# Experts' remainder in units of 64 rows: 14 tiles of 128 rows and 7 of 64 in turns, where 21 tiles of 128 stood

## The reference

```
x = x + tanh(g_xattn) * cross_attention(layernorm(x), ctx)      # |scores|, softmax, 16 heads
logits = layernorm(x) @ w_router                                 # 8 experts
top 2 of softmax(logits) per token, their probabilities as weights
h = gelu(layernorm(x) @ w1[e] + b1[e])                           # 256 -> 1024
y = h @ w2[e] + b2[e]                                            # 1024 -> 256
x = x + tanh(g_ffn) * sum over the two chosen experts of weight * y
```

## Time and profile before

| what | value |
|---|---|
| time, median of 3 runs | 653.47 us (652.01 to 654.26) |
| the profiled execution | 654.93 us, its span 653.1 us |
| PE busy | 633.6 us (97%) |
| DVE, ACT, POOL busy | 459.7, 333.8, 310.7 us |
| mean granted TensorE clock | 0.989 |
| chain of waits, by engine | PE 57%, DMA 3%, DVE 2% |

### The profile page before, as it was taken

The page is one execution under the profiler, slowest core; times in us unless marked ns, Lnnn a source line. Parts: engine busy times, 40 slices in busy tenths (PEclk is TensorE's granted clock), DMA queues, the critical chain, the costliest instruction groups (busy, mean ns, idle before and its releaser), DMA issues.

```text
span 653.1 us, 20940 instructions
## 1 busy us (share of the span) xinstructions
PE 633.6 (97%) x6637; PEld 562.7 (86%) x6638; DVE 459.7 (70%) x1298; ACT 333.8 (51%) x741; POOL 310.7 (48%) x420
## 2 busy tenths in 40 slices
PE   8999999999999999899999999999999999999993
PEld 7799999999999999798888888888888888888872
DVE  5687888888888896689665656556564647777773
ACT  4668777788778875623242323323242324444441
POOL 6423477777777455766352323334242433333333
PEclk9899999999999999899999999999999999999997
DMA  6144354555544445524954333333433344533322
GB/s 208 41 135 156 115 159 153 164 164 177 165 149 132 147 156 172 117 55 81 202 74 60 50 49 49 51 51 58 60 46 56 43 58 54 56 54 52 52 35 25
DMA packets 89157, 63.37 MB, mean 97 GB/s; under 512 B 51489, under 2 KB 84775, under 8 KB 88935
## 3 DMA queue, kind: packets, MB, share of 16 engines
q1 hardware_dynamic: 75519, 43.95, 26.0%
q0 software_dynamic: 13440, 18.14, 16.5%
q10 hardware_dynamic: 104, 0.04, 0.0%
HBM read 28.08 MB, written 24.63 MB: 81 GB/s over the span
## 4 chain that ended last, share of the span: by engine, by line
PE 57%; DMA 3%; DVE 2%; issue 1%; POOLq 0%; ACT 0%; SPq 0%; DVEq 0%; ACTq 0%
PE banks L1720 20%; PE banks L1703 20%; PE banks L1738 7%; PE banks L1752 7%; DMA out_dram<-prob_t,meta 2%; PE banks L1632 1%; DMA x_t<-routed 1%; PE banks L1659 1%; PE banks L1673 0%; PE banks L1613 0%; PE banks L1640 0%; DVE prob L1291 0%; POOLq L681 0%; DVE v_area L1293 0%; DVE top L1091 0%
## 5 line engine op out<-in xcount | busy, mean ns | idle before, releaser
L977 ACT ACTIVATE stage<-banks,bias_t 128x256 f32<-128x256 f32 x200 | 83.8, 470 | 169.6 <-PE banks L1703 157.1
L1703 PE MATMUL banks<-x_t,w_hi 128*128 128x256 f16 x800 | 133.9, 274 | 1.4 <-DMA x_t<-routed 1.4
L1720 PE MATMUL banks<-w,prob 128*128 x800 | 132.4, 273 | 0.6 <-DVE v_area L1293 0.6
L856 POOL DMA_INDIRECT out_dram<-prob_t,meta x46 | 74.7, 1625 | 99.7 <-DVE prob_t L1283 82.6
L1703 PE MATMUL banks<-x_t,w_lo 128*128 128x256 f16 x400 | 109.7, 274 | 0.0
L1720 PE MATMUL banks<-w,v_area 128*128 x400 | 109.1, 273 | 0.0
L1703 PEld LDWEIGHTS banks<-x_t,w_hi 128*128 x800 | 78.5, 98 | 11.1 <-issue 1.5
L986 ACT ACTIVATE stage<-banks,bias_t 128x128 f32<-128x128 f32 x168 | 52.6, 363 | 66.8 <-PE banks L1738 66.5
L1720 PEld LDWEIGHTS banks<-w,prob 128*128 128x128 f16 x800 | 78.1, 98 | 9.8 <-issue 0.8
L819 POOL DMA_INDIRECT routed<-row,pos x64 | 71.2, 1113 | 27.9 <-issue 14.6
L1632 PEld LDWEIGHTS banks<-v_area,prob_t 128*128 128x128 f32 x640 | 73.9, 192 | 4.3 <-DVE attn L1110 0.7
(11 more groups left out here) (254 smaller groups left out, 1254.9 us busy)
## 6 DMA issues: line engine op xcount, KB each, us to landing
stage<-in_L_ffn_w_dram SPq DMA_DIRECT2D x32, 512.0 KB, 4.1
x_in<-in_x_dram SPq DMA_DIRECT2D x16, 256.0 KB, 3.6
x_res<-in_x_dram SPq DMA_DIRECT2D x16, 256.0 KB, 4.0
out_dram<-x_res SPq DMA_DIRECT2D x16, 256.0 KB, 2.9
routed<-turned SPq DMA_DIRECT2D x9, 265.0 KB, 4.8
out_dram<-prob_t,meta POOLq DMA_INDIRECT x67, 3.8
routed<-row,pos POOLq DMA_INDIRECT x64, 2.9
arena<-in_L_ffn_b_dram SPq DMA_DIRECT2D x1, 1024.0 KB, 7.8
```

Of the source, the lines that this page charges most:

```text
L856: pool.indirect_dma_start(out[:, :], bass.IndirectOffsetOnAxis(ap=meta_of(j, pj)[:, b, E:E + 1].bitcast(U32), axis=0), y[:, pj, b], None, ...
L977: ins = act.activation(hid[:, c], H[:, q, c % PER * SLOTS:(c % PER + 1) * SLOTS], ACT.Gelu_apprx_tanh, bias=k.bias_t[:, bass.ds(e * HC + c ...
L1703: mm = pe.matmul(H[:, q, c % PER * SLOTS:(c % PER + 1) * SLOTS], w[:, bass.ds(e, 1), i, c * P:(c + 1) * P].rearrange("p a n -> p (a n)"), ...
L1720: mm = pe.matmul(Y[pj][:, b * D:(b + 1) * D], h[:, pj, c, b * P:(b + 1) * P], w[:, bass.ds(e, 1), c, :].rearrange("p a n -> p (a n)"), sta ...
```

## The change

The remainder is planned in units of 64 rows. There are again 21 small tiles, now in turns of two of 128 rows and one of 64 (tiles 27, 30, 33, 36, 39, 42 and 45 have 64). A 64-row tile is loaded, multiplied, split, finished and scattered with 64 rows; its first layer streams 64 columns, its second layer loads 64 columns of weights and streams w2 as before. The plan fills three groups (25 tiles of 256, 14 of 128, 7 of 64) where it filled two, with 53 counted operations; its second half stands after the split of tile 3 and the finish of tile 1.

```
-SMALL_TILES = (TOKENS * 2 - FULL_TILES * SLOTS) // P + E - 1
+HALF = P // 2
+HALF_TILES = E - 1
+SMALL_TILES = ((TOKENS * 2 - FULL_TILES * SLOTS) // HALF + E - 1 - HALF_TILES) // 2 + HALF_TILES
...
+LATE_SIZES = ((LATE_FULL, SLOTS), (SMALL_TILES - HALF_TILES, P), (HALF_TILES, HALF))
...
+def small_rows_of(tile):
+
+    return HALF if (tile - FULL_TILES) % 3 == 2 else P
...
-        PLAN_OPS = 31
+        PLAN_OPS = 53
...
                 def load_small(t):
...
+                    n = small_rows_of(t)
...
-                    sp.dma_start_transpose(small_rows[p][b], routed.bitcast(F16)[bass.ds(at, P), 0:2 * D])\
+                    sp.dma_start_transpose(small_rows[p][b][:, :, 0:n], routed.bitcast(F16)[bass.ds(at, n), 0:2 * D])\
...
                 def scatter_small(t):
...
-                        out[:, :], bass.IndirectOffsetOnAxis(ap=small_meta(t)[:, E:E + 1].bitcast(U32), axis=0),
-                        y[:, p, 0], None, compute_op=ALU.add).then_inc(small_added[p], 16)
+                        out[:, :], bass.IndirectOffsetOnAxis(ap=small_meta(t)[0:n, E:E + 1].bitcast(U32), axis=0),
+                        y[0:n, p, 0], None, compute_op=ALU.add).then_inc(small_added[p], 16)
...
                 def gelu_small(t, e, q):
...
-                        ins = act.activation(small_part(hid_flat, q)[:, c * P:(c + 1) * P], H[:, q, c * P:(c + 1) * P],
+                        ins = act.activation(small_part(hid_flat, q)[:, c * P:c * P + n], H[:, q, c * P:c * P + n],
...
                 def split_small_hidden(t, q):
...
+                    if small_rows_of(t) == HALF:
+                        part, hi, lo = (x.rearrange("p (c n) -> p c n", c=PER)[:, :, 0:HALF] for x in (part, hi, lo))
...
                 for q in range(HID_BANKS):
                     split_hidden(3, 1, q)
                 finish_rows(1, 0, 1)
+                done(32)
+                dve.wait_ge(plan_consts, 5)
+                dve.tensor_tensor(jump[:], run_base[:, :, 1:E + 1], run_base[:, :, 0:E], ALU.subtract).then_inc(plan, 1)
+                done(33)
+                for g, (tiles, size) in enumerate(LATE_SIZES):
+                    dve.scalar_tensor_tensor(skip[:, g], run_length[:, g], -float(size), jump[:, g], ALU.mult, ALU.add)\
+                        .then_inc(plan, 1)
...
                 def first_small(t, e, c):
...
-                            mm = pe.matmul(H[:, q, c % PER * P:(c % PER + 1) * P],
+                            mm = pe.matmul(H[:, q, c % PER * P:c % PER * P + rows],
...
                 def second_small(t, e, c):
...
-                        mm = pe.matmul(Y[p][:, 0:width], h[p][:, c * P:(c + 1) * P],
+                        mm = pe.matmul(Y[p][0:rows, 0:width], h[p][:, c * P:c * P + rows],
```

More of the change, by code:

```diff
@@ L546, in main_phase @@
         tiles_i = sb("tiles_i", [P, 2, E], I32)
[L547 to L552, removed]
-        plan_place = x_in[:].rearrange("p b t d -> p (b t d)")
-        past = plan_place[:, 0:NT * RUNS].rearrange("p (n r) -> p n r", r=RUNS)
-        packed_row, run_of, skipped, late, row_f, expert_f, halved = (
-            plan_place[:, NT * RUNS + i * NT:NT * RUNS + (i + 1) * NT] for i in range(7))
+        run_length, run_end, jump, skip = (sb(n, [P, 3, E]) for n in ("run_length", "run_end", "jump", "skip"))
+        run_base = sb("run_base", [P, 3, E + 1])
+        spare = sb("spare", [P, 1])
+        plan_place = x_in[:].rearrange("p b t d -> p (b t d)")
+        past = plan_place[:, 0:NT * E].rearrange("p (n r) -> p n r", r=E)
+        packed_row, run_of, skipped, row_f = (
+            plan_place[:, NT * E + i * NT:NT * E + (i + 1) * NT] for i in range(4))
+        late_groups, late_row, late_expert = [], [], []
+        for tiles, size in LATE_SIZES:
+            at = sum(len(range(g.start, g.stop)) for g in late_groups)
+            late_groups.append(slice(at, at + tiles))
+        for kept, views in ((k.row_of, late_row), (k.expert_of, late_expert)):
+            turns = kept[:, FULL_TILES:MAX_TILES].rearrange("p (g k) -> p g k", k=3)
+            views.extend((kept[:, EARLY_TILES:FULL_TILES], turns[:, :, 0:2], turns[:, :, 2]))
         upto, upto_runs = (x_norm[:, i].rearrange("p (n r) -> p n r", r=RUNS) for i in range(2))
@@ L1506, in _ @@
                                   ALU.mult).then_inc(plan, 1)
-                dve.scalar_tensor_tensor(skip[:, E:RUNS], run_length[:, 1], -float(P), jump[:, E:RUNS], ALU.mult, ALU.add)\
+                done(19)
+                dve.tensor_reduce(run_end[:, 1], upto_eight, AX.X, ALU.add).then_inc(plan, 1)
+                done(20)
+                dve.tensor_scalar(run_end[:, 1], run_end[:, 1], float(SMALL_TILES - HALF_TILES), None, ALU.min)\
                     .then_inc(plan, 1)
-                done(19)
@@ L1536, in _ @@
                 finish_rows(1, 0, 1)
+                done(32)
+                dve.wait_ge(plan_consts, 5)
+                dve.tensor_tensor(jump[:], run_base[:, :, 1:E + 1], run_base[:, :, 0:E], ALU.subtract).then_inc(plan, 1)
+                done(33)
+                for g, (tiles, size) in enumerate(LATE_SIZES):
+                    dve.scalar_tensor_tensor(skip[:, g], run_length[:, g], -float(size), jump[:, g], ALU.mult, ALU.add)\
+                        .then_inc(plan, 1)
+                for g, (tiles, size) in enumerate(LATE_SIZES):
+                    dve.tensor_tensor(past[:, late_groups[g]], k.tile_no[:, 0:tiles].unsqueeze(2).to_broadcast([P, tiles, E]),
+                                      run_end[:, g].unsqueeze(1).to_broadcast([P, tiles, E]), ALU.is_ge).then_inc(plan, 1)
+                done(39)
+                dve.tensor_reduce(run_of[:], past, AX.X, ALU.add).then_inc(plan, 1)
+                done(40)
+                for g, (tiles, size) in enumerate(LATE_SIZES):
+                    dve.tensor_tensor(past[:, late_groups[g]], past[:, late_groups[g]],
+                                      skip[:, g].unsqueeze(1).to_broadcast([P, tiles, E]), ALU.mult).then_inc(plan, 1)
+                done(43)
+                dve.tensor_reduce(skipped[:], past, AX.X, ALU.add).then_inc(plan, 1)
+                for g in range(3):
+                    dve.tensor_scalar(late_expert[g], grouped(run_of, g), float(E - 1), None, ALU.min).then_inc(plan, 1)
+                done(44)
+                for g in range(3):
+                    dve.scalar_tensor_tensor(row_f[:, late_groups[g]], packed_row[:, late_groups[g]], run_base[:, g, 0:1],
+                                             skipped[:, late_groups[g]], ALU.add, ALU.add).then_inc(plan, 1)
+                done(50)
+                for g in range(3):
+                    dve.tensor_scalar(late_row[g], grouped(row_f, g), float(E * REGION), None, ALU.min).then_inc(plan, 1)
                 for q in range(HID_BANKS):
@@ L1745, in second_small @@
                 def second_small(t, e, c):
-                    p = t % 2
+                    p, rows = t % 2, small_rows_of(t)
                     if c == 0:
```

91 lines of the change are left out of this document (45 added, 46 removed).

## The result

The changed kernel takes 657.04 us (median of 20 runs, 654.40 to 660.36), the kernel before 654.09 in the runs beside it: 1.0045 times as long, 95% interval 1.0031 to 1.0058. It is slower by about 2.9 us; 651.5, faster by 2.0, was forecast, and the range that was to hold all but 15% ended at 654.4. Much of the spread goes with the mean granted clock: the fastest of the 20 runs had 0.995, the slowest 0.985.

A forecast was written before the change was run, and what follows sets the result against it. The prediction took PE's sequencer, its register operations at 0.662 us per chunk, to bind the small tiles, and scatters the end. From 653.47, 0.6 for the lead and 1.4 in the tail gave 651.5; 649.0 to 654.4 held all but about 15%.

The forecast's parts named there:

- Second layer, "I take 0; the bound is ... 2.8 us lost": Second layer of the seven 64-row tiles on PE: 64-column loads stay hidden, 0 us; at most 2.8 us lost.
- The rival in which the load shows: Second layer of 64-row tiles: a 64-column load at 107 ns costs 2.8 us, ending at 654.3; chance 10%.
- if second-layer pairs after a 128-column matmul start later than 57 ns behind it: Sign of error on PE: the pair's start would lie more than 57 ns behind the first-layer matmul ahead of it.
- the estimate of 53 ns: Second layer of 64-row tiles: by the skill's rule a 64-column load takes 53 ns and just hides.
- First layer, 28 ns: First layer of 64-row tiles on PE: each 64-column matmul takes 28 ns, a step 3.9 instead of 5.28 us.
- "The gain of all tiles before the tail is the lead that was left, once": Small tiles: PE's sequencer, 0.662 us per chunk, binds once its 0.7 us ahead of the array is used; 0.6 us gained.
- "the 64-row steps take about 4 us throughout": Sign of error on PE: steps with a 64-row first layer at about 4 us, where 0.6 to 0.66 per chunk was expected.
- The sum of the forecast: Whole kernel: 0.6 us for the sequencer's lead over the array and 1.4 in the tail, 2.0 us gained.
- The scatters, 0.8 us for one of 64 rows: POOL's scatters at the end: a 64-row one takes 0.8 us less than the 4.55 to 4.59 of 128 rows.
- The plan, 0: DVE's plan, second half 3.8 us, done at 312.9; about 12 us of cover remain before PE needs tile 6's load; 0 us.

The follow-up runs named there:

- fixed experts: The kernel with loads of 128 columns, but PE takes tile number modulo 8 as the expert in small tiles, leaving no register operations there: 644.34 us.
- loads of 128 columns: The changed kernel, but the second layer of a 64-row tile loads 128 columns of the hidden rows, the upper 64 unused: 651.90 us.

## Why the prediction was wrong

- **Second layer, "I take 0; the bound is ... 2.8 us lost".** This step failed, and it alone turns the sign. It was 1.85 us in each of six steps, 11.1 us; on balance it cost 4.7 (131.0 instead of 126.3 from tile 25 to the end), since each slow step let the sequencer get ahead for the next 64-row step. The bound came from twenty fp32 matmuls 107 ns apart, whose loads all have one shape; it bounds how long a load lasts, while the price is that of changing the array's shape between two loads, which the prediction has no term for. No row that I had cited holds such a change. The rival in which the load shows had the sign right and rested on the same wrong quantity. Of the signs of being wrong, "if second-layer pairs after a 128-column matmul start later than 57 ns behind it" is the one that names the place: 0.15 us. The rule of the Trainium skill that I weighed (page "TensorE: Matmul & The Clock Gate", section on weight-path perf modes) and its columns divided by 1.2, which stand in that page's section "LDWEIGHTS (loading the stationary operand)", speak of the load's duration. Where all loads of a step have 64 columns they hide behind matmuls 0.05 us apart, which the estimate of 53 ns allows. The rule that fits the price stood on another page.

The trace of the kernel before does hold changes of shape, by rows, and I didn't read them. In the attention, matmuls with 32 rows of weights (form 32*128, still 128 columns) follow one with 128 rows:

```profile
62.63 0.22 PE L1618 MATMUL banks<-top_t,spread_top 128*128 128x128 bf16 x1
62.79 0.31 PE L1572 MATMUL banks<-arena 32*128 32x154 f16 x8
```

The distance is 0.15 us in 26 of the 30 such places (0.152 here), where the matmul of 128 columns ahead has 0.055 to 0.057 to the one before it. So nearly 0.1 us shows there for one change of shape, and as much on the way back to 128*128; in step 28 it is 0.09 on either side of the pair. The view shows no idle time at this place, though the kernel has a semaphore wait there. That the shape alone makes the distance is argued from its size and its constancy; no run varies it.

- **First layer, 28 ns.** Right: 28 to 29. With fixed experts the whole step takes the array 4.00 us. The prediction's estimate by the Trainium skill (page "TensorE: Matmul & The Clock Gate", section "Back-to-back issue gap"), from about 25 ns for up to 64 columns, was 3.8; the measured distance decides.
- **"The gain of all tiles before the tail is the lead that was left, once".** Right in mechanism, shown by the kernel with loads of 128 columns (a turn of 15.9, a lead of 0.1) and by the one with fixed experts (14.56). In the changed kernel itself it was hidden, since step 28 rebuilds the lead. Line 1799 there, from 546 to 552.7:

```profile
L1799 PEldq FUSED_REGOPS  x10: 46/46/46, 546.1 to 552.5; - x10
...
L1799 PE MATMUL banks<-w,prob x8: 398/403/403, 546.2 to 552.4; 128*64 x8
```

The first operation is 0.1 us ahead of its pair; at the end ten operations are done for eight pairs. The next 64-row step lives on these two chunks. So my sign of error, "the 64-row steps take about 4 us throughout", did appear, though the sequencer was no faster. The sum of the forecast, 2.0 us gained, is what the loads of 128 columns gave: 654.89 to 651.90, by the ratio 2.4 us (1.4 to 3.4), and 2.1 from tile 25's start to the end of the span. That the sum fits so well is partly luck: PE gave 0.9 of it where 0.6 was forecast, with 0.4 in tile 45's own step (5.48 to 5.12) that no term names, and the tail 1.2 where 1.4 was.

- **The scatters, 0.8 us for one of 64 rows.** Right for the chain: 3.84 instead of 4.6. But POOL's instruction is only 0.12 us shorter (1.45 to 1.57); the rest comes from the wait for the landing. From the last scatter's start to the end it is 6.7 us instead of 7.2, so the last one gave 0.5 and not 0.8. In the changed kernel the tail gave 1.4, as the sum had it.
- **The plan, 0.** Right: tile 6's load isn't delayed for PE. The second half took 3.8 us as forecast (309.11 to 312.91). That 312.9 comes out as the time of its end is chance: less the late start it is 310.1, chiefly since the first half is 2.5 us shorter than the whole plan was, which the forecast, as a bound, didn't count.

## What to carry to other kernels

Where two streams share the array, weights of 64 columns in one of them can cost at each change between the two shapes, whatever a load's own duration; if the unused columns can be loaded too, load them. Before such an edit, look in the trace for places where the form of the array changes already, and read the distance there. Before a matmul is made shorter, compare the pace of the register operations that address it with its own: the line's view gives both, and a lead that shrinks says that there is little left to gain. A gain that shows in single steps may be paid for by the step before; only the sum over a whole turn tells.

## What was not expected of the hardware

Changing the load's width between 128 and 64 columns and back costs 0.22 us with two matmuls between; between 128 and 96 it costs nothing. A change from 128 rows of weights to 32 stands with a like distance in the trace of the kernel before, 0.15 us instead of 0.06. A long register operation records 46 ns and a short one 32, yet in most places they keep the sequencer for 124 and 113 ns.
